# Attention entry reordered (first half's q and k first) and its shift turns made fp32r matmuls

## The reference

```python
x = x + 0.5 * _L0_ffn_ref(_layernorm(x), ...)      # ffn0
x = x + _L0_attn_ref(_layernorm(x), ...)           # attn0
x = x + 0.5 * _L0_ffn_ref(_layernorm(x), ...)      # ffn0
x = x + 0.5 * _L1_ffn_ref(_layernorm(x), ...)      # ffn1, 8 experts
x = x + _L1_attn_ref(_layernorm(x), ...)           # attn1
x = x + 0.5 * _L1_ffn_ref(_layernorm(x), ...)      # ffn1

def _L1_attn_ref(hidden, w_dkv, w_q, w_uk, w_uv, w_o):   # 4 sequences of 256 tokens, 16 heads of 16
    c_kv = hidden @ w_dkv.T                              # 256 -> 128
    q = (hidden @ w_q.T).reshape(B, S, HEADS, HEAD_DIM)
    k = (c_kv @ w_uk.T).reshape(B, S, HEADS, HEAD_DIM)
    v = (c_kv @ w_uv.T).reshape(B, S, HEADS, HEAD_DIM)
    scores = jnp.einsum('bqhd,bkhd->bhqk', q, k) * scale + alibi_bias(S)
    attn = jax.nn.softmax(scores, axis=-1)
    out = jnp.einsum('bhqk,bkhd->bqhd', attn, v).reshape(B, S, HIDDEN)
    return out @ w_o.T
```

## Time and profile before

| what | value |
|---|---|
| median of 3 runs | 536.68 us (536.38 to 537.72) |
| the profiled execution | 537.0 us |
| its span, first to last instruction | 535.3 us |
| PE busy | 496.9 us, 93% of the span |
| DVE busy | 387.8 us, 72% |
| ACT busy | 252.5 us, 47% |
| POOL busy | 109.9 us, 21% |
| PE's mean granted clock | 0.982 of full speed |

### The profile page before, as it was taken

The page is one execution under the profiler, slowest core; times in us unless marked ns, Lnnn a source line. Parts: engine busy times, 40 slices in busy tenths (PEclk is TensorE's granted clock), DMA queues, the critical chain, the costliest instruction groups (busy, mean ns, idle before and its releaser), DMA issues.

```text
span 535.3 us, 9081 instructions
## 1 busy us (share of the span) xinstructions
PE 496.9 (93%) x3074; PEld 422.9 (79%) x3074; DVE 387.8 (72%) x1196; ACT 252.5 (47%) x539; POOL 109.9 (21%) x170
## 2 busy tenths in 40 slices
PE   2999999999999999999999995899788989899996
PEld 1788888888888888888888884788666778678885
DVE  4569787664786764788588679878759878638776
ACT  3657543534333434324474345355436766644441
POOL 1001000110100110100002015337503433414452
PEclk9999999999999999999999998899989999899999
DMA  6322310000000000001200000267388430000011
GB/s 205 118 90 77 100 42 1 1 1 1 2 0 1 1 1 1 2 0 41 59 21 1 1 2 1 89 73 125 121 197 262 115 96 2 2 1 1 1 40 39
DMA packets 18797, 25.87 MB, mean 48 GB/s; under 512 B 2848, under 2 KB 12832, under 8 KB 18752
## 3 DMA queue, kind: packets, MB, share of 16 engines
q1 hardware_dynamic: 17696, 24.78, 17.4%
q10 hardware_dynamic: 1056, 0.51, 0.3%
HBM read 17.42 MB, written 5.24 MB: 42 GB/s over the span
## 4 chain that ended last, share of the span: by engine, by line
PE 79%; DVE 10%; issue 3%; ACT 3%; SPq 2%; DMA 1%; POOL 1%; DVEq 0%; ACTq 0%; POOLq 0%
PE ps L578 22%; PE ps L580 21%; PE ps L579 21%; DVE x L1589 3%; PE ps L907 2%; PE ps L593 2%; PE ps L859 2%; PE ps L890 1%; PE ps L980 1%; DVE ps L1672 1%; PE ps L871 1%; DVE tmp L1432 1%; PE ps L888 1%; ACT z L1012 1%; PE ps L969 1%
## 5 line engine op out<-in xcount | busy, mean ns | idle before, releaser
L578 PE MATMUL ps<-zh,w0u_h 128*128 128x512 f32 x256 | 103.2, 403 | 1.5 <-ACT zh L1019 1.5
L580 PE MATMUL ps<-zl,w0u_h 128*128 128x512 f32 x256 | 102.5, 400 | 0.0
L579 PE MATMUL ps<-zh,w0u_l 128*128 128x512 f32 x256 | 102.1, 399 | 0.0
L1041 ACT ACTIVATE gel<-ps 128x512 f32<-128x512 f32 x64 | 38.2, 597 | 104.6 <-PE ps L580 104.5
L1407 DVE TENSOR_TENSOR act<-gel,ps 128x512 f32<-128x512 f32 x64 | 43.7, 683 | 42.5 <-ACT gel L1041 42.4
L578 PE MATMUL ps<-w0d_h,ah 128*128 128x256 f32 x256 | 73.0, 285 | 0.4
L580 PE MATMUL ps<-w0d_l,ah 128*128 128x256 f32 x256 | 71.4, 279 | 0.0
L579 PE MATMUL ps<-w0d_h,al 128*128 128x256 f32 x256 | 71.4, 279 | 0.0
L1589 DVE SCALAR_TENSOR_TENSOR x<-ps,aff,x 128x256 f32<-128x256 f32 x128 | 53.0, 476 | 9.9 <-PE ps L580 8.2
L1047 ACT ACTIVATE ah<-act 128x512 fp32r<-128x512 f32 x64 | 40.3, 629 | 40.4 <-DVE act L1407 40.4
L578 PEld LDWEIGHTS ps<-zh,w0u_h 128*128 128x128 f32 x256 | 48.7, 190 | 12.7 <-ACT zh L1019 1.8
(11 more groups left out here) (182 smaller groups left out, 1041.0 us busy)
## 6 DMA issues: line engine op xcount, KB each, us to landing
stage<-in_w_dram SPq DMA_DIRECT2D x16, 384.0 KB, 3.1
qs<-split_out SPq DMA_DIRECT2D x24, 128.0 KB, 2.8
ks<-split_out SPq DMA_DIRECT2D x48, 64.0 KB, 2.6
stage<-in_w_dram SPq DMA_DIRECT2D x8, 256.0 KB, 2.6
ks<-pad SPq DMA_DIRECT2D x6, 256.0 KB, 9.7
ks<-pad SPq DMA_DIRECT2D x1, 1024.0 KB, 9.3
split_out<-qh SPq DMA_DIRECT2D x4, 256.0 KB, 2.5
split_out<-ql SPq DMA_DIRECT2D x4, 256.0 KB, 3.0
```

Source lines behind the costliest of these rows:

```text
L578: pe.matmul(o, lh, rh, start=start, stop=False, **kw)
L579: pe.matmul(o, ll, rh, start=False, stop=False, **kw)
L580: return pe.matmul(o, lh, rl, start=False, stop=stop, **kw)
L1041: nc.scalar.activation(gel[:, n % 2, :], ps[:, 2 * (n % 2), :], ACT.Gelu_apprx_tanh).then_inc(gelu_s, 1)
```

## The change

Four things. The four transposes of a group in `shift_turn` become plain matmuls in fp32r with an identity in fp32r (`ident_r`), which ACT rounds once into the first quarter of `wr_h` in the stage before. The tile `shift` moves from `macc` to `pad`, in fp32r; its four matrices are now windows that overlap (32 columns apart, 128 wide), of which only the rows 96 to 127 of each result are read, and the memset that clears it waits for the DMAs that read `pad`. In `attn1` on PE, ACT and DVE the first half of heads, q(0,0) and k(0,0), goes before q(0,1) and k(0,1); the statistics of the second block come after k(0,0) on DVE, its normalisation after V's copies on ACT, its transposes after V's projection on PE. SP writes q(0,0) and k(0,0), then q(0,1), reads the first stacks, and writes k(0,1) behind them.

```diff
--- before.py
+++ after.py
@@ -166,7 +166,6 @@
         ks = sb("ks", [P, SLOTS, 2, SEQ], F32R)
         va = sb("va", [P, BT, HEADS, SLOT])
         pbt = sb("pbt", [P, 2, 4, 3 * P])
-        shift = macc[:, :, :].rearrange("p t d -> p (t d)").rearrange("p (s c m) -> p s c m", s=2, c=4)
 
         wa_raw = va[:, :, :, :].rearrange("p t h s -> p (t h s)")[:, 0:WA]
 
@@ -177,6 +176,10 @@
         oth, otl = [[t[:, i, :].rearrange("p (t c q) -> p t c q", t=2, c=KC) for t, i in ((a, 2), (a, 2), (a, 2), (q, 0))]
                     for a, q in ((ah, qh), (al, ql))]
         pad = sb("pad", [P, 2 * SEQ], F32R)
+
+        ident_r = wr_h[:, 0, 0, :]
+        shift = pad[:, 0:2 * (K_ROWS + P)].rearrange("p (s m) -> p s m", s=2)
+        shift_cols = shift[:, :, K_ROWS:K_ROWS + P].rearrange("p s (c m) -> p s c m", c=4)
         mark = sb("mark", [P, 1])
         nmin = sb("nmin", [P, 2, 4, 2])
         rec = sb("rec", [P, 2, HEADS])
@@ -252,6 +255,7 @@
         zero_s = sem("k_stacks_zeroed")
         written_s = [[sem(f"{kind}_written{m}") for m in range(2)] for kind in "qk"]
         rows_s = sem("k_rows_rounded")
+        ident_r_s = sem("ident_rounded")
         pad_zero_s = sem("zeros_ready")
         pad_s = sem("k_rows_spread")
         stack_s = [sem(f"stacks_loaded{i}") for i in range(HALVES)]
@@ -445,9 +449,11 @@
                              pad[K_ROWS:P, :].bitcast(F32).rearrange("p (o q) -> p o q", o=1)
                              .broadcast_to([P - K_ROWS, SLOTS, 2 * SEQ])).then_inc(pad_s, 16)
                 sp.wait_ge(zero_s, 6 * 16)
-                for m, kind in ((0, 0), (1, 0), (0, 1), (1, 1)):
+                for m, kind in ((0, 0), (0, 1), (1, 0)):
                     write(0, m, kind)
-                for h in range(4):
+                read(0)
+                write(0, 1, 1)
+                for h in range(1, 4):
                     read(h)
                 for m, kind in ((0, 0), (0, 1), (1, 0), (1, 1)):
                     write(1, m, kind)
@@ -567,9 +573,11 @@
                     nc.gpsimd.memset(va[:, :, :, :], 0.0).then_inc(wal_s, 1)
                     pool.wait_ge(wal_s, WL + 1)
                     nc.gpsimd.memset(va[:, :, :, HD:HD + 1], 1.0).then_inc(wal_s, 1)
-                    nc.gpsimd.memset(shift[:, :, :, :], 0.0).then_inc(shz_s, 1)
+                    pool.wait_ge(zero_s, 6 * 16)
+                    pool.wait_ge(pad_s, 16)
+                    nc.gpsimd.memset(shift.bitcast(F32), 0.0).then_inc(shz_s, 1)
                     pool.wait_ge(shz_s, 1)
-                    nc.gpsimd.memset(shift[:, :, :, ONE_COL:ONE_COL + 1], 1.0).then_inc(shz_s, 1)
+                    nc.gpsimd.memset(shift_cols[:, :, :, ONE_COL - K_ROWS:ONE_COL - K_ROWS + 1].bitcast(F32), 1.0).then_inc(shz_s, 1)
 
 
         @block.tensor
@@ -756,13 +764,13 @@
                 split_ready(p)
                 project_c(0)
                 project_q(0, 0)
+                project_k(0, 0)
                 project_q(0, 1)
-                project_k(0, 0)
                 pe.wait_ge(acc_s, E * f0 + U1 * st.d1 - 1)
                 project_k(0, 1)
-                transposes(p + 1)
                 project_v(0)
                 project_v(1)
+                transposes(p + 1)
                 split_ready(p + 1)
                 project_c(1)
                 project_q(1, 0)
@@ -860,6 +868,7 @@
 
             def shift_turn(g):
                 if g == 0:
+                    pe.wait_ge(ident_r_s, 1)
                     pe.wait_ge(shz_s, 2)
                     pe.wait_ge(ch_s, 2)
                     pe.wait_ge(cl_s, 2)
@@ -868,7 +877,8 @@
                 if g:
                     pe.wait_ge(sht_s, g)
                 for i in range(4):
-                    mm = pe.transpose(ps[:, 2, i * P:(i + 1) * P], shift[:, g % 2, i, :], ident[:, :])
+                    mm = pe.matmul(ps[:, 2, i * P:(i + 1) * P], shift[:, g % 2, SLOT * i:SLOT * i + P], ident_r,
+                                   start=True, stop=True)
                 mm.then_inc(sht_ps, 1)
 
             def scores_t(hd):
@@ -1130,6 +1140,7 @@
                         if fb == 1 and c == 4 and "attn1" in stages:
                             act.wait_ge(sel_in_s, 32)
                             nc.scalar.activation(pad[K_ROWS:P, :], rows_raw, ACT.Copy).then_inc(rows_s, 1)
+                            nc.scalar.activation(ident_r, ident[:, :], ACT.Copy).then_inc(ident_r_s, 1)
 
             def q_hi(b, m):
                 act.wait_ge(q_ps, 2 * b + m + 1)
@@ -1161,13 +1172,13 @@
                 z_hi(p)
                 c_hi(0)
                 q_hi(0, 0)
+                k_hi(0, 0)
                 q_hi(0, 1)
-                k_hi(0, 0)
                 k_hi(0, 1)
+                v_out(0)
+                v_out(1)
                 normalise(p + 1)
                 z_hi(p + 1)
-                v_out(0)
-                v_out(1)
                 c_hi(1)
                 q_hi(1, 0)
                 k_hi(1, 0)
@@ -1619,11 +1630,11 @@
                 z_lo(p)
                 left_acc(st, 0, 2)
                 left_acc(st, 0, 1)
-                prepare(p + 1, 0)
                 c_lo(0)
                 q_lo(0, 0)
+                k_lo(0, 0)
+                prepare(p + 1, 0)
                 q_lo(0, 1)
-                k_lo(0, 0)
                 k_lo(0, 1)
                 z_lo(p + 1)
                 c_lo(1)
@@ -1675,8 +1686,8 @@
 
             def shifts(g):
 
-                cols = shift[:, g % 2, :, :]
-                return nmin[:, g % 2, :, :], cols[:, :, K_ROWS:K_ROWS + 2], cols[:, :, K_ROWS + 2:K_ROWS + 4]
+                cols = shift_cols[:, g % 2, :, :]
+                return nmin[:, g % 2, :, :], cols[:, :, 0:2], cols[:, :, 2:4]
 
             def shift_hi(g):
                 m, hi, lo = shifts(g)
@@ -1685,12 +1696,12 @@
                     dve.wait_ge(shz_s, 2)
                 if g >= 2:
                     dve.wait_ge(sht_ps, g - 1)
-                V.tensor_copy(hi.bitcast(F32R), m).then_inc(shh_s, 1)
+                V.tensor_copy(hi, m).then_inc(shh_s, 1)
 
             def shift_lo(g):
                 m, hi, lo = shifts(g)
                 dve.wait_ge(shh_s, g + 1)
-                V.tensor_tensor(lo, m, hi, ALU.subtract).then_inc(shl_s, 1)
+                V.tensor_tensor(lo, m, hi.bitcast(F32), ALU.subtract).then_inc(shl_s, 1)
 
             def out_norm(n, t):
                 c = 2 * n + t + 1
```

## The result

The changed kernel has a median of 542.34 us (540.18 to 543.06, four runs) against 536.53 us before: a ratio of 1.0104, 95% interval 1.008 to 1.0127. The forecast was 533.6 us with a range to 536.2, so it missed the sign. The profiled execution has a span of 540.0 us against 535.3, 4.7 us longer, at a mean granted clock of 0.969 of full speed against 0.982.

A forecast was written before the change was run, and what follows sets the result against it. The prediction took the entry to be bound by the stacks' transfer, then by the second block, and the loop by PE. Turns -2.2 and entry -0.9 made -3.1 us, to 533.6 us; own range 532.3 to 535.0, wider 531.8 to 536.2.

The forecast's parts named there:

- Term 1: Head loop's turns: fp32r matmuls save 0.20 us a set of four over 11 sets, -2.2 us; between 0 and -2.8.
- nothing, if four loads in a row can't hide: Turns in the loop: lower bound, no saving, if weight loads pace the set at the present 0.11 us each.
- A third and fourth in the loop: Further stretches at 1.2 GHz in the head loop, where PE is never idle, would cost 1.7 us each.
- slower rival: Attention stage: PE's entry idle lowers the clock for more of the stage, +2.7 us, 539.4 us; chance 0.06.
- Term 2: Attention entry: first minimum +0.2 us, DVE's stalls behind the first minima gone -1.1, together -0.9 us; bounds -1.6 and +1.5.
- if the longer idle of PE: Entry's upper bound, +1.5 us: six of twelve projections at half clock, 1.4 us more, and one DVE stall stays.
- weight loads pace the turns: Rival on the loop's turns: their saving is 0 and the entry's gain stays, 535.8 us; chance 0.14.
- the second block eats the entry's gain: Rival at the entry: statistics 3.05 us later, PE idle, projections at half clock; +1.5 - 2.2, 536.0 us; chance 0.10.

The follow-up runs named there:

- order_filler: Kernel before with the new engine and queue orders, fp32 transposes kept, plus 15 spare matmuls in PE's wait for the second block: 536.68 us, ratio 1.0009.
- turns_mode: Kernel before, its orders kept, with the turns in fp32r issued as transposes instead of plain matmuls: 535.8 us, ratio 1.0002.
- turns_alone: Kernel before with only the fp32r matmul turns (shift in pad, rounded identity), all orders as before: 539.33 us, ratio 1.0057.
- filler: Changed kernel with 15 spare matmuls in PE's wait ahead of the second block's transposes: 537.49 us, ratio 1.0021.
- stats_first: Changed kernel with the second block's statistics put back ahead of c's low half on DVE and its normalisation ahead of V's copies on ACT: 538.41 us, ratio 1.0036.

## Why the prediction was wrong

- **What bounds:** right for the entry (transfer last before, the second block last after) and for the loop (PE). But I took the stage's time at a clock that I let vary only in the entry.
- **Term 1, the turns' pace (failed):** "`L888` starts at 411.56 and the next matmul, whose own 128 weights have to be loaded, at 411.62: 0.06 us a piece. Four make 0.24 instead of 0.44". The 0.06 is one distance in a mixed stream; in a row of four, one turn starts 0.11 behind the other, before and after. And the 0.24 is made of distances of starts, while the 0.44 is a row of the chain that runs to the end of the last turn. From start to start the set had 0.36 and now has 0.39, so the 0.20 saved a set, 2.2 us in all, was nothing, and the groups stayed 3.39 us apart. My bound "nothing, if four loads in a row can't hide" was the case. The rule of the Trainium skill (TensorE: Matmul & The Clock Gate, section LDWEIGHTS), 107 ns for 128 columns, was nearest of the three; the 81 ns of its section Back-to-back issue gap came next, and the halved load of its section on Fast Weight Load didn't show.
- **Term 1, its clock (missed altogether):** the term held the loop's clock at 2.4 GHz, and with the fp32r turns 10.2 us at half clock stand at the loop's start in the profile. By 1.0057 that is +3.1 us where -2.2 was forecast. I had named "A third and fourth in the loop" as part of the slower rival and gave it 0.06, but put it down to PE's wait at the entry; the turns alone do it, with the old entry. Why they do is open.
- **Term 2, the places:** statistics, normalisation, transposes and the first write (381.78) came within 0.3 us of the forecast, the first scores stood behind PE's projections and not behind DMA, and with the clock held the first minimum was at 395.19 (395.8 to 396.6 forecast). The mechanism was right at 2.4 GHz. Its size isn't shown: that profile's span is 1.0 us shorter (0.9 forecast), but over twelve runs the ratio is 1.0009 (0.9991 to 1.0026), which shows no gain.
- **Term 2, the bound (failed):** "if the longer idle of PE (384.9 to 388.8 instead of 2.65 us) puts six of the twelve projections at half clock" stood as an upper bound beside a central case at full clock. PE waited 3.65 us, 1 us more than before, behind which the clock had already fallen in the earlier trace rows; all twelve ran at half (0.43 us apart, 0.19 more each, not the 0.24 of the bound), and the first minimum moved by +2.5 instead of +0.2. In the order alone it moved by 2.3, of which 1.0 came back up to the first `pv`; 1.0041 is +2.2 us where -0.9 was forecast. The row that showed a fall behind 2.65 us of idle should have made this the likeliest case.
- **The sum:** -2.2 - 0.9 forecast; +3.1 and +2.2 measured apart, +5.6 together by the ratio.
- **The rivals:** "weight loads pace the turns" (0.14) and "the second block eats the entry's gain" (0.10) were both right as mechanisms and not exclusive; on top came the slower one (0.06; 539.4 us). Treating them as alternatives kept the slower side too small.

## What to carry to other kernels

Before PE work is taken out or moved, read where PE waits just ahead and what the clock did behind such waits in the trace: here a form of the turns that took no more of PE's time cost 3 us, by a stretch at half clock behind a place where PE waited for DVE. The distance between two matmuls of a mixed stream is no pace for a row of short ones; look for such a row, or take the load as the bound. Compare starts with starts: a row of the chain that ends with an instruction's end is longer than the time for which it holds up the next. Spare matmuls in a wait are a cheap test of whether a loss is a delay or the clock, and with enough of them a small gain of their own.

## What the runs showed of the hardware

- With PE busy for nearly all of the time, the clock stayed at 1.2 GHz in the attention loop for 3.4 us (`order_filler`), 6.8 (`turns_mode`), 10.2 (`turns_alone`, `filler`, `stats_first`) and 13.7 (the changed kernel, 10 of 10 us busy from 410 to 420). Behind the first wait of the kernel before, it was down for 3.4 us.
- The kernel before varies with the clock as well: of the 33 runs beside the first spare matmuls of the loop, those with a mean clock of 0.985 or more had 533.42 to 536.25 us, those at 0.979 to 0.982 had 536.37 to 537.74.
- At full clock a set of four 128x128 turns holds up PE's next matmul for 0.36 us as fp32 transposes, 0.39 as fp32r matmuls, 0.29 as fp32r transposes and 0.81 as fp32 matmuls. The fp32r transposes are the fastest form and were not in the change.
